# A graph-attention kernel on one core: ACT's steps with the one-hot matrix last, and POOL's landing reports behind the third gather

## The reference

```
Wh = (h @ W).reshape(N, 4, 64)
e  = leaky_relu(a_src . Wh[edge_row] + a_dst . Wh[edge_col]);  e = exp(e - max)
alpha = e / segment_sum(e, edge_row)[edge_row]
h_new = segment_sum(Wh[edge_col] * alpha, edge_row) + Wh        # then layernorm, a linear layer, relu
y = Taylor attention of 8 heads with 32 channels:               # "mix"
    sum over nodes of kn x kn x v (kv_mod), kn x v (kv), v      # a sum over all nodes
    then for each node qn x qn against kv_mod, qn against kv, normalised, projected
x = x + gnn(xn) + mix(xn);  x = x + mixture_of_experts(layernorm(x))   # 8 experts, top 2
```

## Time and profile before

| what | value |
|---|---|
| runs of the kernel before, median of 3 | 3717.87 us (3713.49 to 3719.67) |
| the profiled execution: its time / its span | 3726.11 us / 3724.3 us |
| PE busy / weight loads | 2973.9 us (80%) / 2188.1 us (59%) |
| DVE busy | 2657.7 us (71%) |
| ACT busy | 1913.5 us (51%) |
| POOL busy | 2197.9 us (59%) |
| mean granted TensorE clock | 0.895 of full speed |

### The profile page before, as it was taken

How to read it: one execution, slowest core, us unless ns; L and a number is a source line. 1 busy time by engine, 2 the same in 40 slices (tenths; PEclk the granted TensorE clock), 3 DMA queues, 4 the chain that set the end, 5 groups by cost and what they waited for, 6 DMA issues and landing times.

```text
span 3724.3 us, 90309 instructions
## 1 busy us (share of the span) xinstructions
PE 2973.9 (80%) x23065; PEld 2188.1 (59%) x23065; DVE 2657.7 (71%) x6016; ACT 1913.5 (51%) x5687; POOL 2197.9 (59%) x2454
## 2 busy tenths in 40 slices
PE   4878737878877877889999999999976477777995
PEld 2334325545555555567777777777755266666894
DVE  9999997878878878877777777777765644535122
ACT  3777624434444444456666666666643134544663
POOL 4577647777767777776666666666667142244142
PEclk8787868989989989989999999999988768989997
DMA  2222225555555555554444444444444423344264
GB/s 64 87 92 90 80 70 149 139 143 141 136 144 142 141 142 140 141 138 123 120 121 125 120 120 120 120 123 120 121 115 114 146 88 114 105 142 134 93 182 121
DMA packets 324119, 453.01 MB, mean 122 GB/s; under 512 B 79008, under 2 KB 258398, under 8 KB 323736
## 3 DMA queue, kind: packets, MB, share of 16 engines
q0 software_dynamic: 86704, 239.52, 23.8%
q1 hardware_dynamic: 214428, 191.18, 18.5%
q10 hardware_dynamic: 22860, 20.83, 2.1%
HBM read 366.49 MB, written 84.82 MB: 121 GB/s over the span
## 4 chain that ended last, share of the span: by engine, by line
PE 31%; DVE 18%; issue 17%; POOL 14%; DMA 10%; ACT 5%; POOLq 3%; ACTq 2%; DVEq 1%; SPq 0%
POOL room L840 9%; DMA room<-table,room 8%; PE bank L2003 7%; PE bank L2037 5%; DVE room L1358 5%; PE bank L2199 4%; PE bank L2187 4%; DVE room L1357 4%; PE bank L2048 3%; POOL xs_dram L899 2%; POOLq L833 2%; PE bank L1991 2%; ACT room L1128 1%; PE bank L2069 1%; ACTq L1060 1%
## 5 line engine op out<-in xcount | busy, mean ns | idle before, releaser
L840 POOL DMA_INDIRECT room<-table,room x1564 | 1519.7, 972 | 727.3 <-issue 395.1
L2003 PE MATMUL bank<-room 128*128 128x260 f32 x3520 | 947.7, 416 | 255.7 <-DVE room L1543 154.3
L2003 PEld LDWEIGHTS bank<-room 128*128 128x128 f32 x3520 | 686.4, 205 | 382.1 <-issue 282.1
L1543 DVE TENSOR_TENSOR room<-room,bank 128x1024 f32<-128x1024 f32 x440 | 534.9, 1216 | 197.6 <-ACT bank L1073 191.9
L1560 DVE TENSOR_TENSOR room<-bank,room 128x1024 f32<-128x1024 f32 x392 | 477.2, 1217 | 0.0
L1066 ACT ACTIVATE spare<-away,ones 128x512 bf16<-128x512 bf16 x440 | 317.6, 722 | 53.1 <-ACT away L1063 2.3
L1063 ACT ACTIVATE away<-spare,minus_p 128x512 bf16<-128x512 bf16 x440 | 312.8, 711 | 2.1 <-DMA spare<-rows_dram 1.9
L1515 DVE TENSOR_TENSOR room<-iota_f,row_step 128x512 f32<-128x512 f32 x440 | 301.3, 685 | 0.3 <-DVE row_step L1449 0.3
L1073 ACT ACTIVATE bank<-room 128x16 f32<-128x16 f32 x440 | 81.4, 185 | 428.4 <-DVE room L1537 414.4
L1842 DVE TENSOR_TENSOR planes<-bank,spare 128x256 f32<-128x256 f32 x119 | 50.5, 425 | 332.6 <-PE bank L2199 306.1
L2199 PE MATMUL bank<-room 128*128 x952 | 238.1, 394 | 51.2 <-DVE planes L1842 51.0
(11 more groups left out here) (314 smaller groups left out, 4831.8 us busy)
## 6 DMA issues: line engine op xcount, KB each, us to landing
spare<-rows_dram SPq DMA_DIRECT2D x440, 128.0 KB
room<-table,room POOLq DMA_INDIRECT x1564
kv_dram<-room SPq DMA_DIRECT2D x49, 324.0 KB, 2.2
room<-kv_dram SPq DMA_DIRECT2D x196, 81.0 KB
y_dram<-planes SPq DMA_DIRECT2D x119, 128.0 KB, 1.7
room<-xs_dram ACTq DMA_DIRECT2D x110, 128.0 KB, 2.2
q_dram<-room SPq DMA_DIRECT2D x49, 192.0 KB, 1.8
room<-q_dram SPq DMA_DIRECT2D x196, 48.0 KB
```

What stands on the lines that cost most here:

```text
L840: pool.indirect_dma_start(G[:, k.slot, u, :], None, table, bass.IndirectOffsetOnAxis(ap=ixbuf[:, k.slot, u:u + 1].bitcast(I32), axis=0)).t ...
L1543: dve.tensor_tensor(Gw[:, h, :, 0:C].rearrange("p u (h d) -> p u h d", h=GH), G[:, bass.ds(slot, 1), :, 0:C].rearrange("p a u (h d) -> p ( ...
L2003: ins = pe.matmul(pbank[1 + h][:, 0:TW], OH[:, s, u, :], Gw[:, h, u, :], start=(u == 0), stop=(u == U - 1))
```

## The change

In ACT's lap, `copy_oht(k+3)` moves from the beginning of step k to its end, and `copy_yst` moves behind `exps(k+1)`. On POOL the report of group k-1 moves from behind the second gather DMA of group k to behind the third.

```diff
                 pool.indirect_dma_start(G[:, k.slot, u, :], None, table,
                                         bass.IndirectOffsetOnAxis(ap=ixbuf[:, k.slot, u:u + 1].bitcast(I32), axis=0)
                                         ).then_inc(gathered[k.slot], 16)
-                if u == 1 and k.after(1):
+                if u == 2 and k.after(1):
                     report(k + -1)
@@
             for s in range(4):
                 k = At(i, s, 4)
+                if unit is not None:
+                    unit(s)
+                if (k + 1).inside(STEPS):
+                    exps(k + 1)
+                if mode == "q" and s == 0 and not (isinstance(q, int) and q == 0):
+                    copy_yst(q - 1)
+                if mode == "q":
+                    q_part(q, s)
                 if (k + 3).inside(STEPS):
                     copy_oht(k + 3)
-                if unit is not None:
-                    unit(s)
-                if mode == "q" and s == 0 and not (isinstance(q, int) and q == 0):
-                    copy_yst(q - 1)
-                if (k + 1).inside(STEPS):
-                    exps(k + 1)
-                if mode == "q":
-                    q_part(q, s)
```

## The result

The changed kernel takes 3605.28 us in the median of 4 runs (3604.68 to 3605.91), the kernel before 3718.77 us in its 4 (3713.49 to 3719.75): a ratio of 0.9706 with a 95% interval of 0.9694 to 0.9719. That is 113 us, where the prediction had 63 and a range down to 3632. The profiled executions differ by more (spans 3724.3 and 3602.9 us, 121.4 us), because that of the kernel before was 7 us above its median.

A forecast was written before the change was run, and what follows sets the result against it. POOL was taken to bound part K and PE part Q. Terms of -55 + 1.25 + 2 + 2.4 in K, -9 in Q and +0.5 - 5 in the tail gave -62.9 us: 3655 us from 3717.87, 8-in-10 range 3632 to 3702.

The forecast's parts named there:

- Part K: Edge stage's first part, paced by POOL: landing waits saved -55 us, costs +1.25, +2 and +2.4 us.
- landings give way: Rival, 14%: gathers land late, POOL issues earlier and waits as long; 3715 us, or 3695 to 3715 with part of the gain.
- The rule of the Trainium skill: POOL's gathers: 2.0 us + bytes / 436e3, estimated 2.3 us, so every group lands before POOL asks; POOL's part worth nothing.
- The turns: Part K: ACT copies sums after the one-hot matrix, +2.4 us each; 2 us for the first three, +2.4 at the fourth.
- The tail: After part Q: -5 us of POOL's landing waits, +0.5 us for the last copy_yst behind a one-hot matrix.
- Part Q: Second part of the edge stage, taken to be PE's, with one PE-ACT hand-over per lap: -9 us.
- PE's wait for L1147 in that step stays: Part Q, once a lap: PE's wait for ACT's q_part copies stays at 1.07 us, ACT's chain having the same length.
- L1128 behind the exponentials: Part Q: DVE gets weights about 1.3 us earlier once a lap; PE's wait for features shrinks, 9 us, between 0 and 14.8.
- DVE was critical in part Q: Rival, 6%: 1.3 us a lap, 49 times, is 64 us more gain; 3591 us.
- The late unit loads: Rival, 8%: SP's unit loads, issued one step later with a 4.6 us lead, land late; slower, 3725 to 3760 us.
- The late one-hot: Rival, 2%: the one-hot matrix comes late for PE where PE runs without DVE; some 10 us off the gain.
- The forecast of the waits: Part K: POOL's landing waits fall from 82 to some 15 to 25, under 20 us in total.

## Why the prediction was wrong

**Part K, right in its main term.** The sum had -55 + 1.25 + 2 + 2.4 = -49.4 us; K got 1038.5 - 993.6 = 44.9 us shorter. The report alone gave 51.2 of the 53.8 us of its own terms. That landings give way was a rival at 14%, and a fifth of it is true: the waits went, and 13 us came back as longer gather instructions. The rule of the Trainium skill ("DMA: Bandwidth & Descriptors", the anatomy of a DMA on the gpsimd path), by which all landings would have been in before POOL asked, would have made the report worth nothing. The run with the report alone measured 51 us of K, so the waits were the better witness.

**The turns, too small.** They had +4.4 us. With ACT's part alone K grew by 13.0 us, and by 14.5 with the one-hot last alone; beside the moved report it is 6.3 us. At each turn L1173 now begins 2.2 to 2.5 us behind the exponentials instead of 0.2, as foreseen. But the first three turns were not made good: from DVE's last weighing to L1173 all four together took 9.0 and 8.3 us longer in these two runs. That does not settle the cause. Holding the one-hot back made the same stretches 6.8 us shorter than in the changed kernel, and K no shorter, which fits a part whose pace POOL sets. And POOL waited longer for landings, here with ACT's part alone (566 to 1617):

```profile
POOL room L840 <- DMA room<-table,room: 112.4, 100, 4.8
```

This is 82.4 us net, 13.2 more than in the earlier trace rows; with the one-hot alone it is 7.6 more. Why landings come later under ACT's new order, and why less of it is left beside the moved report, stays open.

**The tail, right in the sum.** -4.5 us, measured 167.2 to 162.9, -4.3. The terms were -5 and +0.5 and measured -6.0 with the report alone and +1.7 for ACT's part beside it (+4.4 by itself), so that two misses cancel.

**Part Q, where it failed.** The prediction had -9 us and the runs -67.5. The step that failed is this one: "PE's wait for L1147 in that step stays, since ACT's chain has the same length." ACT's chain from `copy_mix` to L1147 does hold the same instructions, but not the same time, since busy work is not all of its length: the 1.10 us from L1136 to L1061 held a branch and a value load that nothing covered, and without the branch they are 0.73. The chain got 0.59 us shorter and PE's wait for it fell from 1.07 to 0.47 us. The listing of the change showed that the branch had moved behind L1066, and I gave it no price. PE was waiting for this chain once a lap, so that each piece of it counted 48 times.

The terms, from the laps of the single runs: the branch 22.4 - 22.0 = 0.4 us (0.37 in ACT's timeline), 18 us in 48 laps. L1128 behind the exponentials 22.4 - 21.6 = 0.8 us, 36 us: 0.21 in ACT's chain, and some 0.5 from the features that PE no longer waits for at the third step. That one the prediction took for 9 us, by the 14.8 us that the list of waits shows. The list shows only what PE sat idle in 32 laps; the other 16 are the 15 laps whose PE was late by its clock, and the first. The last term is the clock, 15 laps x 1.1 = 16.5 us, which the prediction did not have; either half of ACT's part removes all of it. Together 18 + 36 + 16.5 = 71 us against 67.5 measured; the first and the last lap are shorter than the rest in both kernels (20.7 and 20.0 us before) and gain less.

**The rivals.** "DVE was critical in part Q" at 6% had the time (3591) nearest to the measured one, with half of the mechanism: DVE's earlier exponentials do pay, but only until PE's wait for the features is gone, some 0.5 of the 1.3 us that it assumed, and DVE still waits 104.8 us for them. That 3591 is near is luck: the rest of Q's gain came from ACT's chain and the clock. The late unit loads came about in small: once in the changed kernel, at the fourth turn, where ACT was ready for the load 0.4 us after its issue instead of the 4.6 us that the prediction took for the lead, and it landed after 3.7. DVE's scores were ready there at 1555.95 and the exponentials began at 1556.65, so it cost 0.7 us. The late one-hot did not come about. The forecast of the waits was half right: 51 landing waits and not 15 to 25, nearly all of the usual 0.30 us.

That the fall of the clock comes from PE's waiting is argued from kernels that differ in ACT's order: it fell with 1.54 us of waits a lap and more, in one lap of three or in all, and not with 1.18 us and less. No run changed the waits and nothing else, and why it fell in just one lap of three stays open.

## What to carry to other kernels

Where one engine waits once a lap for a chain on another, price the chain by its timeline from end to end, and look for what is not busy in it: a loop's branch cost 0.37 us there until queued activations covered it. Waits of 1.5 us a lap on a dense PE came with a second loss here, of 1.1 us in each lap in which the clock fell: compare PE's busy time for the same count of matmuls, lap by lap. A list of waits is no upper bound for what an earlier input is worth, when the waiting engine is late in some laps for another reason.

## What the runs showed of the hardware

In part Q the granted clock fell to its lower level for 3.4 us in about every third lap where PE waited 1.07 and 0.47 us in a lap, and in every lap, for some 3.5 and 6.8 us in turn, where it waited 1.3 and 1.28 us or 1.5 and 0.84 us; with 0.71 and 0.47, with 0.84 or with 0.48 us a lap it did not fall. The same kernel took 3714 to 3719 us on some chips and 4707 to 4833 on others, with the idle time in front of instructions that waited for nothing else: 434 gaps in front of L1991 with 350 us in the run with the report alone. There the mean clock was near 0.80 instead of 0.90, and a gain of 113 us became a loss of 78. A gather instruction on POOL took 0.94 us at the least, and some up to 1.5 us. What they took over 0.95 us each grew from 22 to 35 us of part K when POOL waited less between them.
